# An expert layer's first matmuls with the weights staged and held stationary, and GpSimd's slots written out

## The chip, the cores and the metric

The kernel runs on one core of a Trainium2 chip. The metric is the device time of one execution in microseconds (us). The engines are named as the profile names them: PE is TensorE's matmul side, PEld its weight loads, DVE VectorE, ACT ScalarE, POOL GpSimd, SP SyncE; a q behind a name (PEldq, POOLq) is that engine's sequencer.

## What is computed

One transformer block on x of 8 x 256 tokens, 128 channels: cross attention, then a routed feed-forward layer with 8 experts, of which each token uses two. Cut to what matters here:

```python
x = x + xattn(layernorm(x), ctx_2048, ...)            # attention, not touched by the change
h = layernorm(x)
bids = sigmoid(h @ conf_w.T + conf_b) * wealth          # 8 bids for each token
top_bids, selected_experts = top_k(bids, 2)             # two experts for each token
combine = softmax(top_bids)                             # their weights
g = einsum('bsh,ih->bsi', h, gate_w[e])                 # 128 -> 512
u = einsum('bsh,ih->bsi', h, up_w[e])                   # 128 -> 512
expert_out = einsum('bsi,hi->bsh', silu(g) * u, down_w[e])   # 512 -> 128
x = x + sum over the two experts of combine * expert_out
```

All of it is in fp32.

## The kernel before

The program has two parts, one behind the other with a barrier between: `attend` (the first 340 us) and `experts`. The change is in `experts` alone.

`experts` first normalizes x into h, works out the bids and the ranks, and sorts the 4096 picks (2048 tokens times two) by expert into **slots** of 128 rows. A slot belongs to one expert; `SLOTS_PAD` is 40. The results are three tables: `source` (128 x 40, which row of h each lane of a slot takes), `target` (128 x 40, which row of the output buffer in DRAM each lane goes to) and `table` (1 x 40, the expert of each slot). Then comes the stage that the change touches: 40 slots are run through a pipeline over five engines, and at its end the pick outputs are read back (`y_in<-pick_outs`) and summed into x with their weights (`x` L1038), chunk by chunk, and stored.

Each engine has its own copy of the pipeline, written as `step(i, r)` for slot j = 4*i + r. `slots` writes out the first eight steps, puts steps 8 to 35 into a hardware loop of seven turns with four steps each, and writes out the rest. Within a step each engine works on several slots at once (shift -1 is the slot before, +1 the next):

- POOL gathers the rows of slot j+3 from DRAM into `x_in` with an indirect DMA (L855) and scatters the outputs of slot j-2 with another (L879). Its indices come from `source_now` and `target_now`, into which it first copies one column of the tables (L872, L874), since the loop's counter picks that column.
- PE transposes x of slot j+1 (L1105, into `t_ps`); multiplies it with the gate weights (L1113) and the up weights (L1116), with x as the stationary operand and 512 columns of weights as the moving one; runs the second layer of slot j-2 (`down`, L1125) and four transposes of `hidden` of slot j-1 (L1133, into `at_ps`).
- ACT computes silu of the gate half (L907) and copies the transposed hidden rows from `at_ps` to `hiddenT` (L911).
- DVE multiplies silu with the up half (L1018), copies `xT` (L1010) and copies the output of slot j-2 from PSUM (L1026).

PE finds the weights of a slot's expert by loading `table` into a register, L1099, once for the first layer and once for the second. Ahead of the slots PE runs 24 dummy matmuls (`idle`, L1050) while DVE finishes the tables. All buffers between engines are doubled (`x_in` and `y_out` have four), and semaphores say when one is filled and when it is free.

Of the kernel before, what the change touches and what calls it, by code (L numbers as in the profile page):

```python
# [28 lines left out]
P = 128  # L29
# [661 lines left out]
def experts(nc, m, d, out):  # L691
# [9 lines left out]
    with ExitStack() as ctx:  # L701
# [16 lines left out]
        source_copied, target_copied = sem("source_copied"), sem("target_copied")  # L718
# [6 lines left out]
        actT_filled, actT_copied = sem("actT_filled"), sem("actT_copied")  # L725
# [44 lines left out]
        source_now = sb("source_now", [P, 4], mybir.dt.uint32)  # L770
        target_now = sb("target_now", [P, 4], mybir.dt.uint32)
        x_in = sb("x_in", [P, 4, C])
        xT = sb("xT", [P, 2, P])
        silu, hidden = sb("silu", [P, 2, I]), sb("hidden", [P, 2, I])
# [5 lines left out]
        at_ps = [psum(f"at_ps{i}") for i in range(2)]  # L780
# [44 lines left out]
        def _(pool):  # L825
# [33 lines left out]
            def step(i, r):  # L859

                j = 4 * i + r
                before2, before1 = (r - 2) % 4, (r - 1) % 4
                if exists(i, r, 3):
                    pool.wait_ge(xT_filled, j + 1)
                    pool.wait_ge(source_copied, j + 4)
                if exists(i, r, -2):
                    pool.wait_ge(y_copied, j - 1)
                    pool.wait_ge(target_copied, j - 1)
                if exists(i, r, -5):
                    pool.wait_ge(y_stored[before1], (i + (r - 5) // 4 + 1) * 16)  # L870
# [5 lines left out]
                if exists(i, r, 3):  # L876
                    load((r + 3) % 4)
# [5 lines left out]
            for r in range(4):  # L883
                pool.tensor_copy(source_now[:, r:r + 1], source[:, r:r + 1]).then_inc(source_copied, 1)
            pool.wait_ge(source_copied, 3)
            for r in range(3):
                load(r)
# [272 lines left out]
```

## Time and profile before

| | us |
|---|---|
| median of 3 runs | 539.71 (534.32 to 540.8) |
| the profiled execution: its time | 540.74 |
| the profiled execution: its span | 539.1 |
| attention and everything ahead of the slots | 0 to 382 |
| the 40 slots, first gate matmul to first gate matmul of the last slot | 382.57 to 510.74 |
| last slot's rest, read back, sums, store | 510.74 to 539.1 |

In the rows, a line as "t_ps<-down,hiddenT 128*128 x8" is eight matmul instructions that write `t_ps`. An fp32 matmul is recorded as two instructions, each with its weight load on PEld; a transpose is recorded as one. In the brackets at a row's end stands how long the engine sat idle before it and what it was waiting for; "issue" is time in which the trace shows nothing that it waited for.

### The profile page before, as it was taken

Reading aid. Unit: us, or ns where it says so; the run is one execution under the profiler, and the core shown is the slowest. Engines: PE = TensorE matmul, PEld = TensorE weight load, DVE = VectorE, ACT = ScalarE, POOL = GpSimd, SP = SyncE. Lnnn points to the kernel's source line nnn. Section 1 sums busy time; section 2 is a strip of 40 time slices with the busy share of each in tenths; the row PEclk is TensorE's granted clock in tenths of the full one; section 3 lists DMA queues with packets and bytes.
Section 4 is the critical chain, followed back from the end, with each engine's and each line's share of the span. In section 5 each row is a group of like instructions: output and inputs, shape, how many; then the busy total and the mean of one; then the engine's idle time right before and its main releaser. Section 6 shows DMA issues by size and latency. Waiting matters only on the chain. (4 is left out here: it accounts for less than half of the span.)

```text
span 539.1 us, 10943 instructions
## 1 busy us (share of the span) xinstructions
PE 484.7 (90%) x3635; PEld 302.4 (56%) x3636; DVE 356.6 (66%) x646; ACT 289.8 (54%) x584; POOL 181.4 (34%) x381
## 2 busy tenths in 40 slices
PE   2489999999999999999999987988899999999930
PEld 1255555555555555555555544987566666666620
DVE  7798798797888887987889822589143333333316
ACT  1237777777787777777787875310133333333310
POOL 6141231412312412313200001004467666666620
PEclk9999999999999999999999998786999999999985
DMA  6512234333243343332222000800111111111126
GB/s 180 124 43 58 72 84 108 79 107 100 74 125 85 93 121 85 90 81 55 53 63 55 24 2 2 234 1 1 24 36 41 39 39 39 39 43 40 35 83 171
DMA packets 32255, 38.12 MB, mean 71 GB/s; under 512 B 5604, under 2 KB 20580, under 8 KB 32212
## 3 DMA queue, kind: packets, MB, share of 16 engines
q1 hardware_dynamic: 27252, 30.79, 21.1%
q0 software_dynamic: 2560, 5.25, 3.8%
q10 hardware_dynamic: 2400, 1.51, 1.0%
q8 instruction: 27, 0.44, 0.3%
q14 instruction: 16, 0.13, 0.1%
HBM read 16.58 MB, written 4.72 MB: 40 GB/s over the span
## 5 line engine op out<-in xcount | busy, mean ns | idle before, releaser
L463 DVE TENSOR_REDUCE max_part<-max_ps 128x2 f32<-128x1024 f32 (+1 forms) x192 | 226.0, 1221 | 39.1 <-PE max_ps L561 30.8
L422 ACT ACTIVATE probs<-ring_ps 128x512 f32<-128x512 f32 x384 | 198.4, 604 | 50.9 <-PE ring_ps L584 47.7
L584 PE MATMUL ring_ps<-blocks,keys 64*128 64x512 f32 x384 | 151.7, 473 | 2.0 <-ACT probs L422 1.5
L594 PE MATMUL pv_ps<-probs,value_cols 128*32 128x256 f32 x1536 | 103.4, 388 | 0.0
L561 PE MATMUL max_ps<-keys,blocks 64*128 64x512 f32 x256 | 84.3, 448 | 7.5 <-DMA blocks<-masked 6.4
L584 PEld LDWEIGHTS ring_ps<-blocks,keys 64*128 64x128 f32 x384 | 65.6, 187 | 31.5 <-ACT probs L422 25.2
L1018 DVE TENSOR_TENSOR hidden<-up_ps,silu 128x512 f32<-128x512 f32 x40 | 27.7, 692 | 80.9 <-PE up_ps L1116 78.7
L911 ACT ACTIVATE hiddenT<-at_ps 128x512 f32<-128x512 f32 x40 | 23.9, 597 | 75.6 <-PE at_ps L1133 67.0
L338 POOL CAST maxes<-rowmax 128x8 fp32r<-128x8 f32 x32 | 6.3, 197 | 171.2 <-DVE rowmax L470 171.2
L594 PEld LDWEIGHTS pv_ps<-probs,value_cols 128*32 128x32 f32 x1536 | 40.3, 109 | 40.2 <-issue 15.1
L561 PEld LDWEIGHTS max_ps<-keys,blocks 64*128 64x128 f32 x256 | 42.3, 196 | 26.7 <-issue 16.6
L1125 PEld LDWEIGHTS t_ps<-down,hiddenT 128*128 128x128 f32 x320 | 38.9, 192 | 14.1 <-issue 14.1
L566 PE MATMUL max_ps<-keys,blocks 64*128 64x256 f32 x256 | 44.2, 305 | 1.9 <-DVE max_part L463 1.9
L1113 PE MATMUL gate_ps<-gate,xT 128*128 x80 | 42.8, 617 | 3.2 <-DVE xT L1010 2.1
L855 POOL DMA_INDIRECT x_in<-h_rows,source_now x40 | 39.4, 986 | 17.2 <-issue 16.6
L1125 PE MATMUL t_ps<-down,hiddenT 128*128 x320 | 42.7, 277 | 2.2 <-ACT hiddenT L911 1.5
L879 POOL DMA_INDIRECT pick_outs<-y_out,target_now x40 | 39.5, 988 | 12.5 <-issue 9.2
L907 ACT ACTIVATE silu<-gate_ps 128x512 f32<-128x512 f32 x40 | 23.8, 596 | 35.1 <-PE gate_ps L1113 34.5
L1116 PE MATMUL up_ps<-up,xT 128*128 x80 | 40.9, 592 | 0.0
L566 PEld LDWEIGHTS max_ps<-keys,blocks 64*128 64x128 f32 x256 | 33.0, 195 | 12.0 <-issue 4.9
L299 POOL COPY value_cols<-ctx_v_sb 128x128 f32<-128x128 f32 x32 | 10.1, 316 | 55.4 <-PE pv_ps L594 52.4
L1050 PE MATMUL at_ps<-ident 128*128 128x128 f32 x168 | 26.5, 334 | 0.8 <-PEq L110 0.8
(150 smaller groups left out, 492.1 us busy)
## 6 DMA issues: line engine op xcount, KB each, us to landing
keys<-parts SPq DMA_DIRECT2D x96, 96.0 KB
blocks<-masked SPq DMA_DIRECT2D x93, 64.0 KB
ctx_v_sb<-ctx_v_dram SPq DMA_DIRECT2D x8, 256.0 KB, 2.9
gate<-gateT_dram SPq DMA_DIRECT2D x8, 256.0 KB, 2.8
up<-upT_dram SPq DMA_DIRECT2D x8, 256.0 KB, 2.9
y_in<-pick_outs SPq DMA_DIRECT2D x8, 256.0 KB, 5.1
raw<-ctx_kT_dram SPq DMA_DIRECT2D x7, 256.0 KB, 2.7
h_rows<-h SPq DMA_DIRECT2D x4, 256.0 KB, 5.0
```

The lines of the kernel that those rows point to most:

```text
L422: act.activation(probs[par][:, k, PAIR * a:PAIR * (a + 1)], bank("exp", s * XUNITS + u)[:].rearrange("p (g n) -> p g n", n=N), ACT.Exp).th ...
L463: vec.reduce_max(out, bank, axis=AX.X).then_inc(max_done, 1)
L561: mm = pe.matmul(max_ps[w % 2][:, a * BANK:(a + 1) * BANK], blocks[rows, t, g, i * P:(i + 1) * P], keys[rows, t, 0:NC_], start=True, stop= ...
L566: mm = pe.matmul(max_ps[w % 2][:, first:first + N], blocks[rows, t, w - G, i * P:(i + 1) * P], keys[rows, t, NC_:KEYS], start=True, stop=True)
L584: pe.matmul(ps[:], keys[rows, t, k * P:(k + 1) * P], blocks[rows, t], start=True, stop=True)\
L594: mm = pe.matmul(pv_ps[ROWS * g:ROWS * (g + 1), 0:N], value_cols[:, t, k, g, :], probs[q % 2][:, k, g, :], start=(k == 0), stop=(k == KT - 1))
L855: pool.indirect_dma_start(x_in[:, r, :], None, h_dram, bass.IndirectOffsetOnAxis(ap=source_now[:, r:r + 1], axis=0))\
L879: pool.indirect_dma_start(outs_dram, bass.IndirectOffsetOnAxis(ap=target_now[:, before2:before2 + 1], axis=0), y_out[:, before2, :], None) ...
L1018: vec.tensor_tensor(hidden[:, r % 2, :], up_ps[r % 2][:], silu[:, r % 2, :], ALU.mult)\
L1113: pe.matmul(gate_ps[r % 2][:], xT[:, r % 2, :], m.gate[:, bass.ds(e, 1), :].rearrange("p a i -> p (a i)"), start=True, stop=True).then_inc ...
L1116: pe.matmul(up_ps[r % 2][:], xT[:, r % 2, :], m.up[:, bass.ds(e, 1), :].rearrange("p a i -> p (a i)"), start=True, stop=True).then_inc(up_ ...
L1125: mm = pe.matmul(y_ps[:, 0:C], hiddenT[:, r % 2, c, :], down[:, bass.ds(e, 1), c, :].rearrange("p a h -> p (a h)"), start=(c == 0), stop=( ...
```

## The change

**First layer.** The operands change sides. The weights of the slot's expert become the stationary operand, x becomes the moving one, so that the result comes out already transposed: `gate_ps` and `up_ps` now hold 4 blocks of 128 hidden channels, each by 128 tokens. DVE's product goes straight into `hiddenT`, and the four transposes, the bank `at_ps`, ACT's copy and the buffer `hidden` go. Since a stationary operand is now four blocks of weights, each of gate and up is four matmuls of 128 columns in place of one of 512.

**Staging.** ACT copies the expert's gate and up weights (128 x 512 each, found through a `table` load that ACT now makes itself) into a doubled buffer `staged`, one slot ahead. PE's first layer reads `staged` at a fixed address; PE keeps one `table` load for each slot, for `down`.

**Order.** The second layer of a slot comes one step after its first layer and not two; DVE copies `xT` of the next slot ahead of its product and not behind it; the pipeline has 41 steps and not 42.

**GpSimd.** Its 40 slots are written out without a loop, so that both indirect DMAs take their indices straight from a column of `source` or `target`. The column copies and the semaphores around them go; each gather and scatter waits only for its own buffer.

```diff
@@ gpsimd
-            def load(r):
-                pool.indirect_dma_start(x_in[:, r, :], None, h_dram,
-                                        bass.IndirectOffsetOnAxis(ap=source_now[:, r:r + 1], axis=0))\
-                    .then_inc(x_loaded[r], 16)
...
-                if exists(i, r, 4):
-                    pool.tensor_copy(source_now[:, r:r + 1], source[:, bass.ds(j + 4, 1)]).then_inc(source_copied, 1)
-                if exists(i, r, -1):
-                    pool.tensor_copy(target_now[:, before1:before1 + 1], target[:, bass.ds(j - 1, 1)])\
-                        .then_inc(target_copied, 1)
...
-            slots(pool, step, SLOTS_PAD + 2)
+            def load(j):
+                if j >= 4:
+                    pool.wait_ge(xT_filled, j - 3)
+                pool.indirect_dma_start(x_in[:, j % 4, :], None, h_dram,
+                                        bass.IndirectOffsetOnAxis(ap=source[:, j:j + 1], axis=0))\
+                    .then_inc(x_loaded[j % 4], 16)
+
+            def store(j):
+                pool.wait_ge(y_copied, j + 1)
+                pool.indirect_dma_start(outs_dram, bass.IndirectOffsetOnAxis(ap=target[:, j:j + 1], axis=0),
+                                        y_out[:, j % 4, :], None).then_inc(y_stored[j % 4], 16)
+
+            for j in range(3):
+                load(j)
+            for j in range(SLOTS_PAD + 2):
+                if j + 3 < SLOTS_PAD:
+                    load(j + 3)
+                if j >= 2:
+                    store(j - 2)
@@ scalar
+            def stage(j, r):
+                e = act.value_load(table[0:1, bass.ds(j, 1)], min_val=0, max_val=E - 1)
+                wait_for(act, up_filled, j - 1)
+                act.activation(staged[:, r % 2, 0], m.gate[:, bass.ds(e, 1), :].rearrange("p a i -> p (a i)"), ACT.Copy)\
+                   .then_inc(gate_staged, 1)
+                act.activation(staged[:, r % 2, 1], m.up[:, bass.ds(e, 1), :].rearrange("p a i -> p (a i)"), ACT.Copy)\
+                   .then_inc(up_staged, 1)
+
             def step(i, r):
                 j = 4 * i + r
+                if exists(i, r, 1):
+                    stage(j + 1, r + 1)
                 if exists(i, r, 0):
                     act.wait_ge(gate_filled, j + 1)
                     wait_for(act, act_done, j - 1)
                     act.activation(silu[:, r % 2, :], gate_ps[r % 2][:], ACT.Silu).then_inc(silu_done, 1)
-                if exists(i, r, -1):
-                    act.wait_ge(actT_filled, j)
-                    wait_for(act, y_filled, j - 2)
-                    act.activation(hiddenT[:, (r - 1) % 2], at_ps[(r - 1) % 2][:].rearrange("p (c n) -> p c n", n=P),
-                                   ACT.Copy).then_inc(actT_copied, 1)
@@ vector
             def step(i, r):
                 j = 4 * i + r
+                if exists(i, r, 1):
+                    copy_xT(j + 1, r + 1)
                 if exists(i, r, 0):
                     vec.wait_ge(silu_done, j + 1)
                     vec.wait_ge(up_filled, j + 1)
-                    wait_for(vec, actT_filled, j - 1)
-                    vec.tensor_tensor(hidden[:, r % 2, :], up_ps[r % 2][:], silu[:, r % 2, :], ALU.mult)\
+                    wait_for(vec, y_filled, j - 1)
+                    vec.tensor_tensor(hiddenT[:, r % 2].rearrange("p c n -> p (c n)"), up_ps[r % 2][:], silu[:, r % 2, :], ALU.mult)\
                        .then_inc(act_done, 1)
@@ tensor
+            def hidden_rows(ps, weights, x):
+                for c in range(IC):
+                    mm = pe.matmul(ps[:, c * P:(c + 1) * P], weights[:, c * P:(c + 1) * P], x, start=True, stop=True)
+                return mm
+
             def step(i, r):
                 j = 4 * i + r
                 if exists(i, r, 0):
-                    e = expert(j)
                     pe.wait_ge(xT_copied, j + 1)
+                    pe.wait_ge(gate_staged, j + 1)
                     wait_for(pe, silu_done, j - 1)
-                    pe.matmul(gate_ps[r % 2][:], xT[:, r % 2, :], m.gate[:, bass.ds(e, 1), :].rearrange("p a i -> p (a i)"),
-                              start=True, stop=True).then_inc(gate_filled, 1)
+                    hidden_rows(gate_ps[r % 2], staged[:, r % 2, 0], xT[:, r % 2, :]).then_inc(gate_filled, 1)
+                    pe.wait_ge(up_staged, j + 1)
                     wait_for(pe, act_done, j - 1)
-                    pe.matmul(up_ps[r % 2][:], xT[:, r % 2, :], m.up[:, bass.ds(e, 1), :].rearrange("p a i -> p (a i)"),
-                              start=True, stop=True).then_inc(up_filled, 1)
+                    hidden_rows(up_ps[r % 2], staged[:, r % 2, 1], xT[:, r % 2, :]).then_inc(up_filled, 1)
                 if exists(i, r, 1):
                     transpose_x(i, r, 1)
-                if exists(i, r, -2):
-                    e = expert(j - 2)
-                    pe.wait_ge(actT_copied, j - 1)
-                    wait_for(pe, y_copied, j - 2)
+                if exists(i, r, -1):
+                    e = expert(j - 1)
+                    pe.wait_ge(act_done, j)
+                    wait_for(pe, y_copied, j - 1)
```

On PE, one whole step of the slots stands in a row like this before (written out part; TENSOR_LOAD is the `table` load, ISA rows are register work for an address):

```order
L1099 TENSOR_LOAD table
L1099 ISA x2
L1113 ISA [waits silu_done,xT_copied]
L1113 MATMUL gate_ps<-gate,xT 128x512
L1116 REGISTER_ALU [waits act_done]
L1116 MATMUL up_ps<-up,xT 128x512
L1105 MATMUL t_ps<-ident,x_in 128x128 [waits xT_copied,x_loaded3]
L1099 TENSOR_LOAD table
L1099 ISA x2
L1125 ISA [waits y_copied,actT_copied]
L1125 MATMUL t_ps<-down,hiddenT 128x128
```

Three more of the last row's kind follow, and then the transposes of `hidden`, x4. With the change, the step on PE is:

```order
L1098 MATMUL gate_ps<-xT,staged 128x128 [waits silu_done,gate_staged,xT_copied]
L1098 MATMUL gate_ps<-xT,staged 128x128 x3
L1098 MATMUL up_ps<-xT,staged 128x128 [waits act_done,up_staged]
L1098 MATMUL up_ps<-xT,staged 128x128 x3
L1094 MATMUL t_ps<-ident,x_in 128x128 [waits xT_copied,x_loaded3]
L1088 TENSOR_LOAD table
L1088 ISA x2
L1118 ISA [waits y_copied,act_done]
L1118 MATMUL t_ps<-down,hiddenT 128x128
```

The first table load, both wide matmuls and the transposes behind `down` are gone, and `down` now waits for DVE's product itself.

On POOL, one step before, with the two copies and their five waits ahead of both DMAs:

```order
L872 COPY source_now<-source 128x1 [waits target_copied,y_copied,y_stored1,source_copied,xT_filled]
L874 COPY target_now<-target 128x1
L855 DMA x_in<-h_rows,source_now 128x128
L879 DMA pick_outs<-y_out,target_now 9216x128
L872 COPY source_now<-source 128x1 [waits target_copied,y_copied,y_stored2,source_copied,xT_filled]
```

and two steps with the change:

```order
L854 DMA x_in<-h_rows,source 128x128 [waits xT_filled]
L860 DMA pick_outs<-y_out,target 9216x128 [waits y_copied]
L854 DMA x_in<-h_rows,source 128x128 [waits xT_filled]
L860 DMA pick_outs<-y_out,target 9216x128 [waits y_copied]
```

The copies are gone, and the gather no longer stands behind a wait for `y_copied` of its own step.

On ACT, one step with the change (before it was one silu and one copy out of `at_ps`):

```order
L884 TENSOR_LOAD table
L884 ISA x2
L886 ISA [waits up_filled]
L886 ACTIVATE staged<-gate 128x512
L888 REGISTER_ALU
L888 ACTIVATE staged<-up 128x512
L898 ACTIVATE silu<-gate_ps 128x512 [waits act_done,gate_filled]
```

Each silu now has the staging of the next slot ahead of it on ACT's queue.

## Rows read from the trace of the kernel before

**Rows 1.** Windows, the stretch before the slots and the slots; columns as in its head.

```profile
core 0: us, PE busy (x) PEld busy (x) DVE busy (x) ACT busy (x) POOL busy (x), PEclk, DMA share, GB/s
374.00:382.00 8.00, 8.00 (x54) 7.82 (x54) 2.38 (x12) 0.00 (x0) 3.65 (x7) 0.75 0.17 18
382.00:510.00 128.00, 124.15 (x638) 81.66 (x638) 45.01 (x114) 44.27 (x76) 83.09 (x146) 1.00 0.15 38
```

**Rows 2.** Timeline of PE, one slot: start us, us, what [idle before].

```profile
441.12 1.02 PE L1113 MATMUL gate_ps<-gate,xT 128*128 x2
441.98 1.02 PE L1116 MATMUL up_ps<-up,xT 128*128 x2
442.84 0.27 PE L1105 MATMUL t_ps<-ident,x_in 128*128 128x128 f32 x1
442.94 1.06 PE L1125 MATMUL t_ps<-down,hiddenT 128*128 x8
443.84 0.60 PE L1133 MATMUL at_ps<-ident,hidden 128*128 128x128 f32 x4
444.27 1.05 PE L1113 MATMUL gate_ps<-gate,xT 128*128 x2
```

**Rows 3.** Timeline of POOL, one slot.

```profile
442.23 0.98 POOL L855 DMA_INDIRECT x_in<-h_rows,source_now  x1 [0.47 <-issue]
443.51 0.99 POOL L879 DMA_INDIRECT pick_outs<-y_out,target_now  x1 [0.30 <-issue]
444.63 0.18 POOL L872 COPY source_now<-source 128x1 uint32 x1
445.40 0.98 POOL L855 DMA_INDIRECT x_in<-h_rows,source_now  x1 [0.47 <-issue]
```

**Rows 4.** Timeline of PEld and PE, the next slot, at the loop's edge.

```profile
445.79 0.14 PEld L1105 LDWEIGHTS t_ps<-ident,x_in 128*128 128x128 f32 x1 [0.43 <-DMA x_in<-h_rows,source_now]
...
448.62 1.12 PE L1113 MATMUL gate_ps<-gate,xT 128*128 x2 [0.39 <-issue]
```

**Rows 5.** Line L1099, the table load: x count, duration ns min/median/max.

```profile
L1099 PEldq FUSED_REGOPS  x115: 42/151/165, 382.1 to 515.6; - x115
L1099 PEldq TENSOR_LOAD <-table x80: 297/302/497, 381.6 to 515.2; - x80
```

**Rows 6.** Timeline, the first slot's start.

```profile
374.89 7.06 PE L1050 MATMUL at_ps<-ident 128*128 128x128 f32 x48
...
380.41 0.94 POOL L855 DMA_INDIRECT x_in<-h_rows,source_now  x1 [0.30 <-issue]
...
381.79 0.27 PE L1105 MATMUL t_ps<-ident,x_in 128*128 128x128 f32 x1
382.10 0.29 DVE L1010 COPY xT<-t_ps 128x128 f32<-128x128 f32 x1 [5.51 <-PE t_ps L1105]
...
382.57 1.12 PE L1113 MATMUL gate_ps<-gate,xT 128*128 x2 [0.51 <-DVE xT L1010]
```

**Rows 7.** Timeline, the last slot.

```profile
510.74 1.02 PE L1113 MATMUL gate_ps<-gate,xT 128*128 x2
...
518.28 0.29 DVE L1026 COPY y_out<-t_ps 128x128 f32<-128x128 f32 x1 [2.07 <-PE t_ps L1125]
518.85 0.97 POOL L879 DMA_INDIRECT pick_outs<-y_out,target_now  x1 [1.26 <-DVE y_out L1026]
```

**Rows 8.** The chain that ended last: start us, us, what.

```profile
518.85 2.24 DMA pick_outs<-y_out,target_now
```

**Rows 9.** Groups by line and shape, 380 to 515 us: busy us, mean ns | idle before.

```profile
L1018 DVE TENSOR_TENSOR hidden<-up_ps,silu 128x512 f32<-128x512 f32 x40 | 27.7, 692 | 80.9 <-PE up_ps L1116 78.7 <-ACT silu L907 2.2
...
L907 ACT ACTIVATE silu<-gate_ps 128x512 f32<-128x512 f32 x40 | 23.8, 596 | 35.1 <-PE gate_ps L1113 34.5 <-issue 0.3
```

**Rows 10.** DMA queues, 382 to 510 us: packets, MB, share of 16 engines.

```profile
q8 instruction: 2, 0.03, 0.1%
```

**Rows 11.** DMA issues of the page: KB each, median us to landing.

```profile
gate<-gateT_dram SPq DMA_DIRECT2D x8, 256.0 KB, 2.8
```

More of the change, by code:

```diff
@@ L769, in experts @@
         table = sb("table", [1, SLOTS_PAD], I32)
-        source_now = sb("source_now", [P, 4], mybir.dt.uint32)
-        target_now = sb("target_now", [P, 4], mybir.dt.uint32)
         x_in = sb("x_in", [P, 4, C])
         xT = sb("xT", [P, 2, P])
-        silu, hidden = sb("silu", [P, 2, I]), sb("hidden", [P, 2, I])
+        silu, staged = sb("silu", [P, 2, I]), sb("staged", [P, 2, 2, I])
         hiddenT = sb("hiddenT", [P, 2, IC, P])
@@ L779, in experts @@
         gate_ps, up_ps = [psum(f"gate_ps{i}") for i in range(2)], [psum(f"up_ps{i}") for i in range(2)]
-        at_ps = [psum(f"at_ps{i}") for i in range(2)]
+        spare_ps = psum("spare_ps")
         xT_ps, y_ps = t_ps
@@ L907, in step @@
                     act.activation(silu[:, r % 2, :], gate_ps[r % 2][:], ACT.Silu).then_inc(silu_done, 1)
[L908 to L914 removed]
+            act.wait_ge(table_ready, 1)
+            act.wait_ge(m.gate_up_in, 32 * E)
+            stage(0, 0)
+            slots(act, step, SLOTS_PAD)
             n = TILES // CHUNKS
@@ L1016, in step @@
                     vec.wait_ge(up_filled, j + 1)
-                    wait_for(vec, actT_filled, j - 1)
-                    vec.tensor_tensor(hidden[:, r % 2, :], up_ps[r % 2][:], silu[:, r % 2, :], ALU.mult)\
+                    wait_for(vec, y_filled, j - 1)
+                    vec.tensor_tensor(hiddenT[:, r % 2].rearrange("p c n -> p (c n)"), up_ps[r % 2][:], silu[:, r % 2, :], ALU.mult)\
                        .then_inc(act_done, 1)
-                if exists(i, r, 1):
-                    copy_xT(j + 1, r + 1)
-                if exists(i, r, -2):
-                    vec.wait_ge(y_filled, j - 1)
-                    if not isinstance(i, int) or j >= 6:
-                        vec.wait_ge(y_stored[(r - 2) % 4], (i if r >= 2 else i - 1) * 16)
-                    vec.tensor_copy(y_out[:, (r - 2) % 4, :], y_ps[:, 0:C]).then_inc(y_copied, 1)
+                if exists(i, r, -1):
+                    vec.wait_ge(y_filled, j)
+                    if not isinstance(i, int) or j >= 5:
+                        vec.wait_ge(y_stored[(r - 1) % 4], (i if r >= 1 else i - 1) * 16)
+                    vec.tensor_copy(y_out[:, (r - 1) % 4, :], y_ps[:, 0:C]).then_inc(y_copied, 1)
             copy_xT(0, 0)
-            slots(vec, step, SLOTS_PAD + 2)
+            slots(vec, step, SLOTS_PAD + 1)
             for t in range(TILES):
@@ L1049, in idle @@
                 for _ in range(turns):
-                    pe.matmul(at_ps[0][:, 0:P], m.ident[:], m.ident[:], start=True, stop=True)
+                    pe.matmul(spare_ps[:, 0:P], m.ident[:], m.ident[:], start=True, stop=True)
             idle(20)
@@ L1128, in step @@
                     mm.then_inc(y_filled, 1)
-                if exists(i, r, -1):
-                    pe.wait_ge(act_done, j)
-                    wait_for(pe, actT_copied, j - 2)
-                    for c in range(IC):
-                        mm = pe.transpose(at_ps[(r - 1) % 2][:, c * P:(c + 1) * P],
-                                          hidden[:, (r - 1) % 2, c * P:(c + 1) * P], m.ident[:])
-                    mm.then_inc(actT_filled, 1)
             transpose_x(0, 0, 0)
-            slots(pe, step, SLOTS_PAD + 2)
+            slots(pe, step, SLOTS_PAD + 1)
 def kernel(x, ctx_2048, L0_xattn_w_qkv, L0_xattn_w_proj, L0_xattn_b_proj, L0_ffn_conf_w, L0_ffn_conf_b,
```

29 lines of the change are left out of this document (3 added, 26 removed).

## Prediction, made before the changed kernel ran

> **What bounds the kernel now.** I read the windows first, then one slot's timeline on each engine, then both ends of the slots. The windows say where to look: over the 128 us of the slots PE is busy for 124, at a granted clock of 1.00 (the upper of its two levels, 2.4 GHz) [rows 1]; DVE and ACT are busy for a third of it, POOL for two thirds. The reader is to see that PE has next to no idle time there, and that a second engine may be as full without showing it, since the time between two indirect DMAs isn't counted as busy.
>
> PE's timeline gives one slot as a sum of start-to-start times [rows 2]: gate 0.86, up 0.86, transpose of x 0.10, down 0.90, transposes of hidden 0.43, together 3.15 us. POOL's is as long: gather, scatter, two copies and the gaps, 442.23 to 445.40, 3.17 us, all its gaps "issue" [rows 3]. From the first gate matmul, 382.57 [rows 6], to that of the last slot, 510.74 [rows 7], are 128.17 us or 39 periods of 3.286. So 0.13 us for a slot are above PE's floor. One slot shows where some of it goes: the gather lands late, PE waits 0.43 for it, and the next gate matmul waits again for PE's own queue, which could not run ahead past that wait (448.62 is 4.35 after 444.27) [rows 4]. Two engines set the pace together, each with some 3.16 of 3.29.
>
> **PE's part of the change.** Gate and up become two groups like down: 4 matmuls, 8 recorded instructions, 128 columns, fp32. Down's group takes 0.90 for 8 (442.94 to 443.84) [rows 2]; the 48 dummy matmuls are of the same form and give a second reading, 7.06 us, though half of them ran at the lower clock level [rows 1, 6]. So gate and up cost 2 x 0.90 in place of 2 x 0.86, +0.08; the 16 weight loads in place of 4 hide beside the matmuls as down's 8 do. The transposes go, -0.43. New floor: 0.90 + 0.90 + 0.10 + 0.90 = 2.80; with down's pitch taken more closely, 0.112 for an instruction, it is 24 x 0.112 + 0.11 = 2.79.
>
> **Does anything make PE wait?** Call T the start of the transpose of slot j's x. DVE's copy of `xT` starts 0.31 after it and the gate matmul can start 0.78 after it (381.79, 382.10, 382.57) [rows 6]. In the new order the copy is ahead of DVE's product, so this holds in every step, and PE is busy until T + 0.10 + 0.90 = T + 1.00 with down. Slack 0.22. Down of slot j-2 needs a product that was done 2 us earlier. PE's queue has one table load for a slot in place of two: 0.30 and 0.15 with gaps around them [rows 5], some 0.7 in all, between the transpose and down, and it can run while gate and up are in the array. It costs nothing as long as the queue is 0.7 ahead.
>
> **ACT's part.** ACT gets two copies of 128 x 512, SBUF to SBUF, and a table load, and loses one copy from PSUM. No row shows a copy of that size from SBUF; the nearest are ACT's passes over 128 x 512 from PSUM, 0.60 [rows 9]. The bounds: 0.3 (half) below, twice that, 1.2, above; I take 0.60, the row of the same size and type. ACT's round from the start of one silu to the next is then: table load beside the silu, 0.8, two copies 1.2, handover 0.1, together 2.1. PE's period is 2.79, so 0.7 is spare; the copies would have to take 0.95 each to set the pace. They are staged one slot ahead: the staging of slot j+1 starts once up of slot j-1 is done, ends about 1.4 later, and is needed 3.8 later. The silu of slot j queues behind it and can't start before its gate matmul is done, 1.9 after T plus 0.2, where staging has been done since T + 1.4. The cover is 0.7 at each place; gone, the excess goes into every slot.
>
> **DVE's part.** Product 0.69 [rows 9], two copies of 0.29 [rows 6, 7], as before, some 1.5 of 2.79 with handovers. No cost, no gain.
>
> **POOL's part.** Gather 0.98 and scatter 0.99 remain [rows 3]. Back to back without copies an indirect DMA has 0.30 ahead of it (the scatter and the third gather) [rows 3, 6], behind copies 0.47. So its period becomes 1.97 + 0.60 = 2.57, at worst 1.97 + 0.94 = 2.91. I take 2.57, since the row with 0.30 is the one without a copy ahead. Gathers no longer stand behind the wait for the step's own output and run up to three slots ahead, so that such late landings end. The scatter waits for `y_copied`, and behind it on POOL stands a gather with over 4 us to spare.
>
> **Start.** Gathers start about 0.9 earlier, and it gains nothing: PE runs its dummy matmuls until the transpose at 381.79 anyway (374.89 + 7.06 less the last one's tail) [rows 6]. The first period has no down in it: gate and up 1.80, then 0.78 from the transpose to the gate matmul, 2.58. The 38 others take 2.79. The last gate matmul is then at 382.57 + 2.58 + 38 x 2.79 = 491.17, against 510.74: **-19.6**.
>
> **End.** Now 8.11 lie between the last gate matmul and the last scatter (518.85) [rows 7]. Then: gate and up 1.80; last up result 0.15 later, DVE's product 0.69 with 0.1 of handover, done at 2.74; down starts at 2.85 and is readable 1.05 later, 3.9; DVE copies it until 4.25; the scatter follows 0.28 later, if POOL is free. It isn't quite: the scatter ahead of it starts at about 3.45 and ends at 4.43, so 4.75. That is **-3.4**: the transposes, ACT's copy of them and two of the handovers are gone. What follows is the same: landing 2.24 after the scatter [rows 8], read back, sums, store.
>
> **Sum.** -19.6 - 3.4 = -23.0. Against the profiled execution, 540.74 (span 539.1 and 1.6 around it), that gives 517.7. The median of the three runs is 539.71, 1.0 lower: 516.7, so **517 us**, 4.2% below.
>
> **Rivals.**
> *GpSimd sets the pace.* If each indirect DMA costs the gap of 0.47, its period is 2.91, 0.12 above PE's: 38 x 0.12 = +4.6, 521.5. For it: POOL was level with PE before. Against: the gaps of 0.30 [rows 3, 6].
> *PE's or ACT's queue sets the pace.* If the table load behind the transpose isn't hidden on PE, some 0.3 of 0.7 shows in each slot, period 3.09, +11: 528. Against it: the same load stood there before, and down followed the transpose at once (442.84, 442.94) [rows 2]; for it, the slot behind the late gather, where PE's queue showed after a wait [rows 4].
> *It moves nothing.* Both paces stay, since late landings were the cause and not POOL's copies: PE falls to 2.79 but waits for gathers. POOL's own length forbids it unless landings slow down; about 537.
> *Slower: instructions are fetched anew.* PE's loop of four steps grows from 4 x 34 to 4 x 50 matmuls and weight loads. During all turns of the loop the q8 instruction queue brought 2 blocks in 128 us [rows 10], so the present loop stays resident. If the longer one doesn't, each of seven edges stalls PE for a fetch. The nearest price is a load's 2.8 us to landing [rows 11]; one block for each edge gives 7 x 2.8 = +20, 537; two blocks give +39, 556. It decides from the length at which the loop no longer fits.
> The rule for this stands in the Trainium skill, "Runtime: NRT & Kernel Launch", Instruction fetch mechanics: blocks of 256 instructions, only two held, and a taken branch outside them waits for a fetch. By that rule a body of some 260 PE instructions, 200 of them matmuls and loads, could span three blocks and thrash. The present body, over 136 and under 256, touches two, and the trace agrees that it isn't fetched again; for a longer one no row here decides. It is what speaks most against this change.
>
> **How the numbers follow.** Forecast 0.70; GpSimd's pace 0.12; a queue's pace 0.07; nothing moves 0.04; slower 0.07 (0.06 refetching, 0.01 copies above 1.3 us on ACT). Some of the slower cases' weight, one block for an edge, is within 2%. A measurement of this kernel tells from no change about 2%, which is 529. So faster 0.87, same 0.08, slower 0.05. The range for 8 in 10: low, 511.5, is the fastest run before, 534.3, less 23; high, 527, takes in GpSimd's pace with the spread of the runs and most of the queue's.
>
> **What would show it.** In the changed trace: gate-to-gate starts 2.8 apart, groups of 8 at 0.90 for gate, up and down; `xT` copied ahead of the product; POOL's gaps at 0.30 or put down to DVE's y_out, none of PE's waits to DMA x_in; ACT's staging at 0.6 each; the last scatter about 23 earlier. Wrong would be: PE waiting for `staged`, or for issue after each transpose; POOL without waits at 2.9; more than 3 or 4 blocks on the q8 instruction queue inside the slots; a clock below 1.00 there.

## The result, and the profile after

The changed kernel took **516.4 us** (median of 4 runs, 514.65 to 518.94) beside 537.2 us of the kernel before (4 runs, 534.32 to 540.8). The ratio is 0.960, with a 95% interval of 0.954 to 0.966: faster, by 20.8 us in the medians. That is what the prediction was made for, and it stands for that occasion. The kernel before stands 2.6 us lower here than in the table that the prediction started from (539.71), because a fourth run, of 534.59, has joined the three. On a later occasion the same code, unchanged, took 543.6 us beside 540.5; experiments 5 and 7 to 12 are about that, and the result can't be carried further without them.

The profiled execution took 514.65 us, with a span of 512.9. The windows, columns as in [rows 1]:

```profile
core 0: us, PE busy (x) PEld busy (x) DVE busy (x) ACT busy (x) POOL busy (x), PEclk, DMA share, GB/s
382.00:490.00 108.00, 107.81 (x966) 107.81 (x967) 46.02 (x116) 66.95 (x115) 71.34 (x73) 1.00 0.16 45
```

PE has no idle time left, and its weight-load side is now as full as its matmul side (it was 81.66 of 128 in [rows 1]). The timeline of one slot, all engines, where [rows 2, 3] had PE's and POOL's:

```profile
439.87 0.27 PE L1094 MATMUL t_ps<-ident,x_in 128*128 128x128 f32 x1
439.98 1.06 PE L1118 MATMUL t_ps<-down,hiddenT 128*128 x8
440.16 0.63 ACT L886 ACTIVATE staged<-gate 128x512 f32 x1 [0.39 <-PE up_ps L1098]
440.18 0.29 DVE L999 COPY xT<-t_ps 128x128 f32<-128x128 f32 x1 [1.51 <-PE t_ps L1094]
440.24 0.97 POOL L854 DMA_INDIRECT x_in<-h_rows,source  x1 [0.30 <-PE t_ps L1094]
440.38 0.68 DVE L1009 TENSOR_TENSOR hiddenT<-up_ps,silu 128x512 f32<-128x512 f32 x1
440.69 0.62 ACT L888 ACTIVATE staged<-up 128x512 f32 x1
440.87 1.06 PE L1098 MATMUL gate_ps<-xT,staged 128*128 128x128 f32 x8
441.16 0.29 DVE L1015 COPY y_out<-t_ps 128x128 f32<-128x128 f32 x1
441.73 0.98 POOL L860 DMA_INDIRECT pick_outs<-y_out,target  x1 [0.53 <-DVE y_out L1015]
441.76 1.06 PE L1098 MATMUL up_ps<-xT,staged 128*128 128x128 f32 x8
441.96 0.60 ACT L898 ACTIVATE silu<-gate_ps 128x512 f32<-128x512 f32 x1 [0.65 <-PE gate_ps L1098]
442.65 0.27 PE L1094 MATMUL t_ps<-ident,x_in 128*128 128x128 f32 x1
```

The reader sees down 0.89, gate 0.89, up 0.89 and the transpose 0.11, together 2.78 from 439.87 to 442.65. DVE's copy of `xT` starts 0.31 after the transpose, PE is covered by down for 1.00, and the gate matmul has no wait behind it. ACT's second copy starts 0.53 after its first. POOL waits for others' results in both its gaps.

The start and the end, where [rows 6] and [rows 7, 8] had them, first the two ends of the timeline and then the chain of waits:

```profile
372.13 7.03 PE L1039 MATMUL spare_ps<-ident 128*128 128x128 f32 x48
378.99 0.27 PE L1094 MATMUL t_ps<-ident,x_in 128*128 128x128 f32 x1
379.65 1.16 PE L1098 MATMUL gate_ps<-xT,staged 128*128 128x128 f32 x8 [0.38 <-DVE xT L999]
...
488.28 1.06 PE L1098 MATMUL gate_ps<-xT,staged 128*128 128x128 f32 x8
...
490.33 0.69 DVE L1009 TENSOR_TENSOR hiddenT<-up_ps,silu 128x512 f32<-128x512 f32 x1 [1.55 <-PE up_ps L1098]
491.17 0.29 DVE L1015 COPY y_out<-t_ps 128x128 f32<-128x128 f32 x1
491.70 1.15 PE L1118 MATMUL t_ps<-down,hiddenT 128*128 x8 [0.58 <-DVE y_out L1015]
492.89 0.29 DVE L1015 COPY y_out<-t_ps 128x128 f32<-128x128 f32 x1 [1.44 <-PE t_ps L1118]
493.46 0.97 POOL L860 DMA_INDIRECT pick_outs<-y_out,target  x1 [0.76 <-DVE y_out L1015]
```

```profile
493.46 2.25 DMA pick_outs<-y_out,target
```

Where the 26.1 us between the two profiled executions (540.74 and 514.65) went, by differences of these starts:
- **Between the gate matmuls of the first and the last slot**: 108.63 in place of 128.17, -19.5. Of the 39 periods 37 are 2.79; the first is 2.55, the second 2.89.
- **From the last gate matmul to the last scatter**: 5.18 in place of 8.11, -2.9.
- **Ahead of the first gate matmul**: 379.65 in place of 382.57, -2.9. This isn't the change's. Between 334 and 354 us both kernels run the same code, and PE's clock drops twice to its lower level, for 6.8 us each time in the profile of before and for 3.4 us each in this one. The two windows with the lower level in them, of before:

```profile
334.00:338.00 4.00, 3.53 (x16) 3.56 (x17) 3.68 (x24) 1.28 (x1) 2.59 (x13) 0.50 0.17 49
...
347.00:352.00 5.00, 5.00 (x26) 5.00 (x26) 2.56 (x4) 0.85 (x2) 0.00 (x0) 0.52 0.17 51
```

and of the changed kernel:

```profile
334.00:338.00 4.00, 3.60 (x19) 3.63 (x19) 3.68 (x25) 1.28 (x1) 2.58 (x13) 0.57 0.22 42
...
347.00:352.00 5.00, 5.00 (x32) 5.00 (x32) 4.36 (x6) 0.31 (x1) 0.00 (x0) 0.66 0.18 54
```

Experiment 10's kernel, which differs from the changed one in PE's loop alone, was caught with the 6.8 us of before both times, and its first gate matmul stands at 382.53, where before had 382.57.

- **Behind the last scatter**: 19.4 in place of 20.3 to the span's end, -0.8; the code there is the same, and no row says what shortened it.

So 22.4 us are the change's, and some 3.7, by this reading, the difference of two executions.

### The profile page after: what moved, and what is told of

It reads as the page before. It is cut to its first block and busy times, and to the rows that moved or that the text cites. A ratio compares the mean times of both kernels' runs of the same rounds, so it can differ in the third digit from the quotient of the medians.

```text
span 512.9 us, 11298 instructions
## 1 busy us (share of the span) xinstructions
PE 463.4 (90%) x3955; PEld 324.2 (63%) x3956; DVE 357.1 (70%) x646; ACT 313.2 (61%) x625; POOL 168.6 (33%) x301
## 3 DMA queue, kind: packets, MB, share of 16 engines
HBM read 16.58 MB, written 4.72 MB: 42 GB/s over the span
## 5 line engine op out<-in xcount | busy, mean ns | idle before, releaser
L999 DVE COPY xT<-t_ps 128x128 f32<-128x128 f32 x40 | 11.7, 292 | 67.2 <-PE t_ps L1094 67.2
L860 POOL DMA_INDIRECT pick_outs<-y_out,target x40 | 39.4, 985 | 28.7 <-DVE y_out L1015 28.7
L854 POOL DMA_INDIRECT x_in<-h_rows,source x40 | 38.9, 972 | 20.9 <-PE t_ps L1094 11.5
L886 ACT ACTIVATE staged<-gate 128x512 f32 x40 | 25.3, 631 | 31.5 <-DVE table L986 17.4
L1098 PE MATMUL gate_ps<-xT,staged 128*128 128x128 f32 x320 | 42.5, 276 | 0.8 <-DVE xT L999 0.8
L1098 PE MATMUL up_ps<-xT,staged 128*128 128x128 f32 x320 | 42.3, 275 | 0.0
L1098 PEld LDWEIGHTS gate_ps<-xT,staged 128*128 128x128 f32 x320 | 38.9, 192 | 1.2 <-DVE xT L999 1.2
L1098 PEld LDWEIGHTS up_ps<-xT,staged 128*128 128x128 f32 x320 | 38.9, 192 | 0.0
```

Source lines behind the costliest of these rows:

```text
L854: pool.indirect_dma_start(x_in[:, j % 4, :], None, h_dram, bass.IndirectOffsetOnAxis(ap=source[:, j:j + 1], axis=0))\
L860: pool.indirect_dma_start(outs_dram, bass.IndirectOffsetOnAxis(ap=target[:, j:j + 1], axis=0), y_out[:, j % 4, :], None).then_inc(y_stored ...
L886: act.activation(staged[:, r % 2, 0], m.gate[:, bass.ds(e, 1), :].rearrange("p a i -> p (a i)"), ACT.Copy)\
L1098: mm = pe.matmul(ps[:, c * P:(c + 1) * P], weights[:, c * P:(c + 1) * P], x, start=True, stop=True)
```

## The experiments

Each edit is to the changed kernel unless it says otherwise. Medians stand with the kernel before beside them.

**1. GpSimd's part alone.** The kernel before, with its GpSimd block replaced by the changed kernel's:

```
-            slots(pool, step, SLOTS_PAD + 2)          # copies of indices, loop
+            for j in range(SLOTS_PAD + 2):            # load/store from source[:, j:j + 1]
+                if j + 3 < SLOTS_PAD:
+                    load(j + 3)
+                if j >= 2:
+                    store(j - 2)
```

> The kernel before with GpSimd's written-out slots alone. Theory (two engines set the pace, PE 3.15 and POOL 3.17 for a slot): POOL falls to about 2.6 and waits for y_out, PE goes to its own floor, 3.16 for a slot with some of its loop edge left, 39 x 0.12 = about 4.5 us less, 0.991 of before, no wait of PE for x_in. Rival (PE alone set the pace, with its own queue at the loop's edge): the period stays at 3.25 to 3.29 and the time within 1 us of before.

534.4 us (531.01 to 537.58) beside 539.9: ratio 0.988 [0.979, 0.997]. From the first to the last gate matmul 123.88 us in place of 128.17, periods of 3.12 to 3.25 and none longer, where before had single ones of 3.4 to 4.3. So with PE's old order GpSimd's part is worth 4.3 us, and it is single long slots that go. They aren't all slots with a late landing. Six of the seven periods over 3.3 us in the profile of before stand four apart (the 13th, 17th, 21st and so on to the 33rd), where PE's loop branches back, and the landing of [rows 4] falls on the longest of them. The loop is still in this kernel, and its gathers now start 6.4 us ahead of their transpose in place of 3.9 (medians from the sixth slot on). That PE's queue, with its gathers there in time, is far enough ahead to hide the branch fits both, but no run separates the two.

**2. Everything but GpSimd's part.** The changed kernel with the loop and the index copies of before on GpSimd:

```
+                if exists(i, r, 4):
+                    pool.tensor_copy(source_now[:, r:r + 1], source[:, bass.ds(j + 4, 1)]).then_inc(source_copied, 1)
+                if exists(i, r, -1):
+                    pool.tensor_copy(target_now[:, before1:before1 + 1], target[:, bass.ds(j - 1, 1)])\
+                        .then_inc(target_copied, 1)
```

> The changed kernel with GpSimd's slots as before (loop, column copies). Theory: POOL paces alone, 3.17 for a slot and 0.5 more at each loop edge, 3.29 in the mean, so that the slots take 128 us as before, PE idles 0.4 to 0.5 a slot waiting for x_in, and only the end gives its 3 us: 0.995 of before. Rival (POOL was level only because it was driven by PE's pace): slots at 2.8 to 2.9, the time as the changed kernel's, 0.96.

518.5 us (515.51 to 519.12), ratio 0.961 [0.954, 0.968]: the whole gain. The gate matmuls are 2.79 apart from the third slot on and take 108.63 us in all. My theory, that POOL would pace at 3.29, fell. POOL's timeline there:

```profile
440.60 0.98 POOL L855 DMA_INDIRECT x_in<-h_rows,source_now  x1 [0.33 <-issue]
441.89 0.99 POOL L879 DMA_INDIRECT pick_outs<-y_out,target_now  x1 [0.31 <-issue]
442.88 0.20 POOL L872 COPY source_now<-source 128x1 uint32 x1
443.01 0.18 POOL L874 COPY target_now<-target 128x1 uint32 x1
443.34 0.99 POOL L855 DMA_INDIRECT x_in<-h_rows,source_now  x1 [0.15 <-issue]
```

The same instructions as in [rows 3] repeat after 2.74 us instead of 3.17 (every fourth time after 2.92, so that the mean is PE's 2.79). In the kernel before, the gather had 0.47 of "issue" ahead of it and the first copy 0.13; here 0.15 (0.33 where it took 2.92) and nothing. Those gaps were POOL following PE's pace and not its own length. The profile puts no name of another engine to them, but DVE's rows give it, since the first copy waits for `y_copied`. The copy that raises it, of before and of this kernel:

```profile
444.13 0.29 DVE L1026 COPY y_out<-t_ps 128x128 f32<-128x128 f32 x1
```

```profile
442.05 0.29 DVE L1034 COPY y_out<-t_ps 128x128 f32<-128x128 f32 x1
```

In before it ends at 444.42, and POOL's first copy starts 0.21 later [rows 3]. That distance is 0.20 to 0.29 in all 33 steps between 385 and 505 us. Here it ends at 442.34, while POOL is still busy with its scatter, and the first copy starts the moment the scatter ends.

**3. The copies without the loop.** As experiment 2, with GpSimd's steps written out:

```
-            slots(pool, step, SLOTS_PAD + 2)
+            for j in range(SLOTS_PAD + 2):
+                step(*divmod(j, 4))
```

> The changed kernel with GpSimd's slots written out, but with the column copies and their semaphores kept. Theory: a POOL step is still gather, scatter, two copies and gaps, 3.1 to 3.17, without the loop edges: slots 39 x 3.15 = 123 us, about 14 above the changed kernel, 0.985 of before. Rival (the loop's edge and its register work are what cost, the copies are small): period below 2.95, under 522 us.

518.7 us (516.27 to 519.12), ratio 0.959 [0.952, 0.966], slots 108.63 us: neither the copies nor the loop of GpSimd cost anything once PE runs in the new order.

**4. DVE's order.** The product goes back ahead of the copy of `xT`:

```
-                if exists(i, r, 1):
-                    copy_xT(j + 1, r + 1)
                 if exists(i, r, 0):
                     ...
+                if exists(i, r, 1):
+                    copy_xT(j + 1, r + 1)
```

> The changed kernel with DVE's product ahead of its xT copy, as before. By the prediction's count the gate matmul may start 0.78 after the transpose where DVE is free and is due 1.00 after it; with the product ahead it is ready at 0.25 + 0.60 + 0.28 + 0.18 = 1.3: PE waits 0.3 a slot for xT, 12 us in all, about 528. Rival (the order is free, since the product has long ended): no change, 516.

531.7 us (527.27 to 532.82), ratio 0.983 [0.975, 0.992]. The slots take 121.70 us, 13.1 more than in the changed kernel, periods 3.09 to 3.19. In the timeline the transpose is still followed at once by down, but `xT` starts 0.86 after it instead of 0.31, and PE waits:

```profile
441.22 0.27 PE L1094 MATMUL t_ps<-ident,x_in 128*128 128x128 f32 x1
441.33 1.06 PE L1118 MATMUL t_ps<-down,hiddenT 128*128 x8
441.48 0.69 DVE L1007 TENSOR_TENSOR hiddenT<-up_ps,silu 128x512 f32<-128x512 f32 x1 [1.76 <-PE up_ps L1098]
442.08 0.28 DVE L999 COPY xT<-t_ps 128x128 f32<-128x128 f32 x1
442.42 0.97 PEld L1098 LDWEIGHTS gate_ps<-xT,staged 128*128 128x128 f32 x8 [0.22 <-DVE xT L999]
```

So the place of one line on DVE carries 13 of the 19.5 us that the slots gained: the slack of 0.22 us exists only with the copy first.

**5. Two more copies on ACT**, and **6. four more**, each 128x512 from the weights in SBUF to a buffer that nothing reads (2, then 4):

```
+                wait_for(act, again_done, 2 * j)
+                for k in range(2):
+                    act.activation(again[:, k], m.gate[:, bass.ds(e, 1), :].rearrange("p a i -> p (a i)"), ACT.Copy)\
+                       .then_inc(again_done, 1)
                 act.activation(staged[:, r % 2, 0], ...
```

> The changed kernel with two more copies of 128 x 512 on ACT in each staging, into a buffer that nobody reads. By the prediction's sum (table load 0.8 beside the silu, copies one behind the other, handover 0.1) ACT's round would be 3.1 to 3.2 and set the pace, +13 us. By the trace of the changed kernel the table load is hidden behind the wait for up_filled and copies follow each other every 0.54: round 4 x 0.54 + 0.6 = 2.76, just below 2.79, 0 to +2 us.

> The same with four more copies. By the trace's count the round is 6 x 0.54 + 0.6 and a handover = 3.9 to 4.0, +1.15 a slot, +45 us. By the prediction's sum, 0.8 + 6 x 0.6 + 0.1 = 4.5, +67 us.

Two more: 547.9 us (546.61 to 548.41) beside 540.5, ratio 1.013 [1.010, 1.017]. Neither theory gave that, and the periods don't fit any: 2.79 and 2.89 as in the changed kernel, with one of 4.2 to 5.3 about every third. Where no such stretch falls, four copies fit into a slot without a cost. Four more: 543.6 us in a single run, with no such stretch: periods of 3.60 (3.46 to 3.74 from the third on). Both expectations, 3.9 and 4.5, were too high. Its ACT timeline shows the round:

```profile
441.40 0.59 ACT L904 ACTIVATE silu<-gate_ps 128x512 f32<-128x512 f32 x1
441.88 2.20 ACT L890 ACTIVATE again<-gate 128x512 f32 x4
443.96 0.63 ACT L892 ACTIVATE staged<-gate 128x512 f32 x1
```

Each copy takes 0.52 of ACT from start to start (0.63 by its own duration, which overlaps the next one), silu 0.48, and the table load adds nothing to be seen: 6 x 0.52 + 0.48 = 3.60. With two copies the round is 1.52, not 2.1 as I had it, and with four 2.56, below 2.79.

**7. Two banks for y.** Down of slot j no longer waits for the copy of slot j-1's output, and there are two dummy matmuls fewer ahead of the slots:

```
-        xT_ps, y_ps = t_ps
+        xT_ps, y_ps = t_ps[0], [t_ps[1], spare_ps]
...
-                    wait_for(pe, y_copied, j - 1)
+                    wait_for(pe, y_copied, j - 2)
```

> The changed kernel with down's result alternating between two banks, so that the last down does not wait for the copy of the one before it, and two dummy matmuls fewer ahead of the slots. Last down starts 0.5 earlier, and the last scatter behind it 0.3 to 0.5; the first transpose starts 0.4 earlier, if its gather has landed. Under 1 us in all, not to be told from no change by the time, but in the trace.

546.0 us (545.39 to 548.16), ratio 1.011 [1.007, 1.016], with the same stretches as experiment 5, so the time tells nothing of the banks, nor of the two dummy matmuls. The end does, in the timeline:

```profile
519.71 1.06 PE L1098 MATMUL gate_ps<-xT,staged 128*128 128x128 f32 x8
...
522.58 1.15 PE L1118 MATMUL spare_ps<-down,hiddenT 128*128 x8
522.59 0.29 DVE L1015 COPY y_out<-t_ps 128x128 f32<-128x128 f32 x1
...
524.43 0.97 POOL L860 DMA_INDIRECT pick_outs<-y_out,target  x1 [0.30 <-DVE y_out L1015]
```

The last down starts 2.87 after the gate matmul, beside the copy and not behind it, and the last scatter 4.72 after it in place of 5.18.

**8. A longer loop on PE.** Eight steps a turn in place of four, some 520 instructions in place of 260:

```
-            slots(pe, step, SLOTS_PAD + 1)
+            for j in range(8):
+                step(*divmod(j, 4))
+            with pe.Fori(1, 4) as k:
+                for s in range(8):
+                    step(2 * k + s // 4, s % 4)
+            for j in range(32, SLOTS_PAD + 1):
+                step(*divmod(j, 4))
```

> The changed kernel with eight steps in a turn of PE's loop in place of four, three turns (400 matmuls and weight loads a turn). Theory (loop edges cost nothing, and what was fetched stays): the same time within 1 us, the q8 queue brings one to three blocks more in the slots, all hidden. Rival (a body that spans more than two blocks is fetched anew on each turn): two or three edges with a stall of 3 us or more, +6 to +17 us, and six or more blocks in the slots.

546.3 us (545.77 to 546.51), ratio 1.011 [1.007, 1.014]. The stretches begin in the fourth period (2.54, 2.89, 2.79, then 4.18), where this kernel's instructions are still those of the changed one, and where experiments 5 and 7 have theirs too (4.25, 4.19). Three different edits and one pattern speak against the edits as its cause; experiments 9 and 10 test that. Experiments 5 to 8 ran together; 1 to 4 had run together earlier, with nothing of the kind.

**9. The changed kernel again**, nothing altered, and **10. the longer loop again** beside it.

> The changed kernel, nothing altered. Three kernels that differ from it in small ways (two more copies on ACT, a longer loop on PE, two y banks) took 546 us on one chip, with stretches of 1.4 to 2.2 us about every third slot in which the counts that PE raises reach DVE and ACT up to 2.9 us late. Theory 1: this belongs to the chip those ran on, whenever PE has no gaps. Then this kernel gives either 516 us (a period of 2.79 us in all slots) on a chip like the first, or 546 us with the same stalls on a chip like that one, and the long loop beside it gives the same as this one. Theory 2: it belongs to the three edits. Then this kernel gives 516 us and the long loop 546 us, side by side.

> The changed kernel with eight of PE's steps to a turn of its loop in place of four (about 520 instructions a turn against 260). Theory 1 (the stalls belong to the chip): the same time as the changed kernel beside it within 0.5%, 516 or 546 us. Theory 2 (they belong to the edit, PE's instructions of a longer turn being fetched anew): 546 us where the changed kernel gives 516 us. In the trace of the queue that brings instructions: with theory 1 the count of its packets in the slots may rise, but no period over 2.9 us follows one.

The changed kernel: **543.6 us** (10 runs, 538.29 to 545.33) beside 540.5 (19 runs), ratio 1.006 [1.001, 1.011]. The longer loop: 543.7 us (540.31 to 545.7), ratio 1.008 [1.004, 1.013]. So the stretches aren't the edits', and theory 2 fell for both. But theory 1 fell in its word "chip" as well: these two ran on the chip of experiments 1 to 4. It is a condition that comes and goes with the occasion. None of the ten runs was near 516, and the kernel before was the same as ever in it. From the first to the last gate matmul are 134.10 us in place of 108.63; 14 of the 39 periods are over 3.3, most of them 4.1 to 5.0, and hold 24.1 of the 25.5. The first one, on the timeline of experiment 9:

```profile
387.60 1.06 PE L1098 MATMUL up_ps<-xT,staged 128*128 128x128 f32 x8
...
388.50 0.27 PE L1094 MATMUL t_ps<-ident,x_in 128*128 128x128 f32 x1
...
388.60 1.06 PE L1118 MATMUL t_ps<-down,hiddenT 128*128 x8
...
390.45 0.29 DVE L999 COPY xT<-t_ps 128x128 f32<-128x128 f32 x1 [3.25 <-remote]
390.50 0.63 ACT L886 ACTIVATE staged<-gate 128x512 f32 x1 [1.66 <-remote]
...
390.79 1.16 PE L1098 MATMUL gate_ps<-xT,staged 128*128 128x128 f32 x8 [1.13 <-DVE xT L999]
```

The matmuls are on record at their usual pitch, yet DVE starts `xT` 1.95 after the transpose (0.31 in an undisturbed slot), and ACT its staging 1.7 late. The view of waits has "remote" for it, no engine of this core that it could name. By the trace's semaphore events, the count for up arrives at 390.39, that for the transpose at 390.42 and that for down at 390.52: within 0.13 us, though down's eight matmuls alone need 0.89 of PE. Had PE run its matmuls late, one after the other, the last would have come 0.9 after the others; that is an argument, since a matmul's end is modelled in the trace and only its start is on record. In the result's trace every such count comes 0.29 after its last matmul's start; here 56 of some 150 on record come over 0.6 after it, the latest 2.8. I call these late counts. The queue that brings instructions had 3 packets in the slots in experiment 9 and 5 in experiment 10:

```profile
q8 instruction: 3, 0.05, 0.1%
```

One thing does tell the occasions apart, and it is in the traces themselves: records are missing. The 80 indirect DMAs raise their counts 1280 times in all. Of these updates 1280 are on record in the result's trace and 1269 to 1280 in those of experiments 1 to 4, but only 622 to 677 in those of experiments 5 to 12, while the other DMAs' 4256 are complete in every trace. The views of DMA issues show it as a missing time to landing, first in the result's trace and then in experiment 9's:

```profile
pick_outs<-y_out,target POOLq DMA_INDIRECT x38, 2.3
```

```profile
pick_outs<-y_out,target POOLq DMA_INDIRECT x37
```

Two of the traces with such gaps have no stretch of late counts: experiment 6's (651 on record; one count late, no long period), and the one of the kernel before from which [rows 1] to [rows 11] were read (700). So what loses the records isn't enough to make counts late; it needs a kernel like the changed one. It also leaves a rival that no run here tests: counts may come late because they are being recorded. Every time given here is of an execution with at least its span and clock on record.

**11. Two more copies again**, and **12. the product first again** beside it.

> The changed kernel with two more copies of 128x512 on ACT in each slot. The changed kernel itself has by now taken 516 us at one time and 543 us at another (stretches of 1.3 to 2.2 us about every third slot in which PE's counts reach DVE and ACT late), so this run says first which of the two holds here. Without those stretches: by the trace's pitch of 0.52 to 0.54 us a copy, four copies and SiLU keep ACT for 0.60 + 3 x 0.53 + 0.48 = 2.7 us of a slot of 2.79, so 517 us and periods of 2.79; by the prediction's sum (0.95 us to spare, two copies 1.05 to 1.2) a period of 2.9 to 3.05 and 520 to 526 us. With them: 547 us again and the same stalls.

> The changed kernel with DVE's product ahead of its copy of the next transposed rows, which gave periods of 3.09 to 3.19 us and 531.7 us before. If the run beside it (two more copies) is without stalls, this one repeats 532. If the run beside it has them, theory 1: they come because the weight-load side of PE is never idle for a slot's length (100% of the slots in the changed kernel, 91% here, 81% with four more copies, 64% in the kernel before, the last two having none), and 91% is still too much: stalls here too, an average period near 3.45 us, 545 us. Theory 2: any gap in a slot is enough: 532 us and no period over 3.3 us.

548.4 us (542.65 to 548.79) beside 541.8, ratio 1.013 [1.008, 1.017], and 549.0 us (542.76 to 551.01), ratio 1.015 [1.010, 1.021]. The condition still held, and PE's gap of 0.3 in each slot doesn't help: the order that gave 531.7 us in experiment 4 has periods of 3.09 with single ones of up to 5.5 in it, 138.34 us from the first to the last gate matmul, a mean of 3.55. Experiment 11 shows the ACT round with four copies once more, 2.55 from start to start and no wait between them:

```profile
383.75 1.14 ACT L890 ACTIVATE again<-gate 128x512 f32 x2
...
385.83 0.58 ACT L904 ACTIVATE silu<-gate_ps 128x512 f32<-128x512 f32 x1
386.30 1.14 ACT L890 ACTIVATE again<-gate 128x512 f32 x2
```

## Why the prediction was right, and where not

- **PE's floor: right.** 24 x 0.112 + 0.11 = 2.79 was the period, to the hundredth. The groups take 0.89 rather than 0.90.
- **Nothing makes PE wait: right.** The gate matmul of [rows 6] waited 0.78 after the transpose; in the new order down covers 1.00 of it. Experiment 4 takes the cover away and pays 13 us. The one table load for a slot shows nowhere.
- **First period, 2.58: measured 2.55. Slots, -19.6: measured -19.5.** The second period was 2.89 where the sum had 2.79; no step of the prediction has those 0.10.
- **Start, no gain from earlier gathers: right.** The dummy matmuls end at the transpose, 378.99, as before. That all of it stood 2.9 earlier was the other execution's clock.
- **End, -3.4: measured -2.9.** The mis-sized term is the last down. I had it 2.85 after the last gate matmul; it started 3.42 after it, behind DVE's copy of the slot before out of the one y bank (491.17, then 491.70). I had priced down's operand and not its destination. With two banks (experiment 7) it starts after 2.87 and the scatter after 4.72, where I had 4.75.
- **ACT's sum: too high, without a consequence.** 0.60 for a copy was right as a duration (0.63 and 0.62) and wrong as a price: back to back each costs 0.52, and the table load shows nowhere. The round is 1.52 and not 2.1. The copies could have taken 1.15 each, and not 0.95, before ACT set the pace ((2.79 - 0.48) / 2).
- **"Two engines set the pace together": wrong.** PE's own length did, with the long slots on top. POOL's 3.17 of [rows 3] shrank to 2.74 with every instruction in place (experiments 2 and 3), which is below PE's new 2.79. GpSimd's part is worth 4.3 us alone and nothing beside the rest. The sum came out all the same, because it took POOL's new period as below PE's in any case: for this part of the change that was luck.
- **The rivals.** GpSimd's pace, 521.5, and a queue's, 528, didn't occur. Nor did the fetching: 3 packets on the instruction queue from 382 to 490 us where [rows 10] had 2, in the result's trace, the last of them at 423.6, so none in the last six turns of the loop. With a loop twice as long there were 5, none between 465 and 508 us, in which most of its third and last turn falls, and 543.7 us beside 543.6 for the shorter one. The rule from the Trainium skill that the prediction feared, "Runtime: NRT & Kernel Launch" (Instruction fetch mechanics), that only two blocks of 256 instructions are held, would give both loops fetches at their turns; the counts, and the clean 2.79 at every turn of the result's trace, speak against it. The same section has another figure for PE, room for 2048 instructions. The traces agree with that one: by it both loops stay in place.
- **What no step had.** The late counts cost 25.5 us and undo the gain on three of the five occasions on which kernels of the new order ran. Nothing in the profile of before points to them, and the predicted 517 holds for the occasions without them: 516.4, and 518.5 and 518.7 in experiments 2 and 3. That the result fell on such an occasion was luck.

What stays open is the cause of the late counts. Shown: they come with the changed kernel as it is, and on another chip with three variants of it; a longer loop, another order on DVE, two copies more on ACT or a y bank more neither bring them about nor end them. A gap of 0.3 in a slot doesn't stop them, and in the single run with one of 0.8 (experiment 6, run beside 5) there is one late count and no long period. The kernel before took the same time on all occasions (medians 537.2 to 541.8). That they need PE's weight-load side to be nearly full (91% or more of the undisturbed slots in the kernels that have them, 81% in experiment 6, 64% before) is an argument from these few and not shown. What differs between the occasions shows in the traces only as the missing records of experiment 9; what causes it isn't seen.

No version beat both kernels in both conditions. Without late counts the changed kernel is the fastest of those run; with them, the kernel before.

## What to carry to other kernels

A gap labelled "issue" need not be the engine's own length while another engine as full as it sets the pace. Look up what the instruction behind the gap waits for, and see whether it starts at a fixed distance from the one that raises that count, as POOL's copy did (0.20 to 0.29 behind DVE's copy of y, in every step). Price back-to-back work by its spacing, not by its duration. For the last slot ask of each instruction what its destination waits for, and not only its operands: buffers that are free in the steady state aren't at the end. And a gain measured on one occasion wants a second look on another, above all where a change fills an engine completely; it was -4% and +0.6% here for the same code.

## What the runs showed of the hardware that I had not expected

- On some occasions PE's counts reach DVE and ACT up to 2.9 us after the matmul, several within 0.13 us, about every third slot, with PE's own records at their usual pitch. In some of the slots after it PE's clock fell to its lower level for 3.4 us (459.4 and 483.3 us in experiment 9), which no undisturbed trace shows inside the slots.
- On those occasions about half of the indirect DMAs' 1280 count updates are missing from the trace (622 to 700 on record), in kernels with and without late counts; on the others at most 11 are.
- ACT's passes over 128x512 from SBUF take 0.63 us each and start 0.52 apart.
- An indirect DMA on GpSimd follows a copy after 0.15 us at the least and another indirect DMA after 0.30; the copy costs 0.13 from start to start (experiment 2).
- Between attention and the slots the clock's lower stretches lasted from 3.4 to 13.7 us, with all but the same code that far, and the first gate matmul of the slots stands between 378.1 and 384.0 us in the traces. The runs of the kernel before lie between 535.0 and 541.8 us beside experiment 9.
